# The normaliser multiplied onto q, the KV product added to the lepe sum in PSUM, and the work placed anew

## The chip, the core and the metric

The kernel runs on one core of a Trainium2 chip. A core has TensorE for matrix products (PE in the profile), VectorE (DVE), ScalarE (ACT), GpSimd (POOL) and SyncE (SP), which only issues copies here. SBUF holds operands, PSUM the sums of TensorE. Every engine works through its own list of instructions in order; semaphores connect the lists. The metric is the device time of one execution in microseconds (us).

## The reference

All data is fp32. `x` is [8, 128, 16, 16]: 8 batches, 128 channels, T = 256 positions. Two layers follow each other, each with a group norm before it and a residual around it. The first is linear attention with a gate:

```
q, k, v, o = split(w_qkvo @ gn(x) + b)               # 128 channels each, 8 heads of 16
lepe = depthwise 5x5 conv of v + b_lepe
q, k = elu(q) + 1, elu(k) + 1
k    = k * softmax(mean(q) . k) * T
z    = 1 / (q . mean(k) + 1e-6)
kv   = rope(k)^T v / T
res  = (rope(q) @ kv) * z + lepe
x    = x + w_proj @ (res * o) + b_proj
```

The second is a Mamba block on the normalised x: a projection, a causal convolution over 4 positions, and a selective scan with 16 states for each of 64 inner channels, in four groups of channels:

```
h[t] = exp(delta[t] * A) * h[t-1] + delta[t] * u[t] * B[t];   y[t] = sum over states (h[t] * C[t]) + D * u[t]
x    = x + proj(layernorm(y * silu(z) @ W_out + skip * gn(x)))
```

## The kernel before

The scans set the frame. A batch has 8 units g = 0 to 7, each a tile of 128 x 1024 (4 groups of channels times 256 positions on the free axis). Per unit VectorE forms `DB` = du * Bs in PSUM (L1174) and scans it with the decay `dec` (L1199) into `hst`; GpSimd multiplies `hst` by `Cs` (L958); ScalarE makes `dec` two units ahead from the copies `dlt` (L843); TensorE sums `hst` over the states into Y ("collect", L573 and L583). In the last two batches scan and products run in halves. `du` is spread over the partitions by a matmul (L556) at the start of a batch's units 0 and 4; `Bs`, `Cs` and `dlt` are spread by copies through DRAM scratch that SyncE issues (L264, L272). After unit 7's collect VectorE gates the sum: `y` (L1144), in the middle of the next batch's unit 1.

All the rest of the work is woven into the units. It is written as short generators, one for each stage and engine: `front` (q, k, v, o, softmax, normaliser, rope, KV), `lepe` (the 5x5 convolution, 32 matmuls of L430 on four shifted copies `V` of v), `mid` (result, projection, group norm, layer norm: `xl`, `XN`), `tail` (Mamba projections up to `delta` and `du`), `back` (output projection: `xl2` L1147, X L827, the store L303). While batch b is scanned, `back` runs for b-1, `tail` for b+1, `mid` for b+2, `front` and `lepe` for b+3. A `yield n` in a generator is the place, in quarters of a unit (0 to 31), at which its next step is issued; these numbers alone set the order on each engine. Batches 1 to 4 are a loop of two pairs. For the first batches, which have no period before them, the tables `places` give the positions: below 100 before the first scan, 100 to 132 inside batch 0, above it between batch 0 and batch 1. Steps with equal places keep the order back, tail, mid, front, lepe.

The steps that the change touches: `QR` (L707) is the rotated q, copied from PSUM; `lz` and `zS` (L708, L711) the normaliser 1/(...) as exp(-ln); `KVM` (L1081) the masked KV; L440 multiplies KVM by QR into F1[:, T:2T]; VectorE then forms `u1` (L1090) = that times zS, and `u2` (L1094) = lepe in F1[:, 0:T] + bias + u1; GpSimd gates, `u3` = u2 * o (L922); L444 and L447 add X and the projection in PSUM. On the way to the layer norm of `back`: L536 the sum, L815 its square, L540 the variance, L818/L821 ln and exp (`rr2`), L1147 `xl2`, L544/L546 the output.

Of the kernel before, what the change touches and what calls it, by code (L numbers as in the profile page):

```python
# [7 lines left out]
ALU = mybir.AluOpType  # L8
# [39 lines left out]
def block_kernel(nc, x, w0, w1, cc, out):  # L48
    with ExitStack() as ctx:
# [33 lines left out]
        QR = [sb(f"QR_{j}", [P, T]) for j in range(2)]  # L83
        lz, zS = sb("lz", [P, T]), [sb(f"zS_{j}", [P, T]) for j in range(2)]
        KVT, KVM = sb("KVT", [P, 4, P]), [sb(f"KVM_{j}", [P, P]) for j in range(2)]
        u1, u2, u3 = sb("u1", [P, T]), sb("u2", [P, T]), sb("u3", [P, T])
# [123 lines left out]
        def _(sp):  # L210
# [10 lines left out]
            def front(b, j):  # L221

                yield 6
                sp.wait_ge(S("vpad_ready"), b + 1)
                sp.dma_start(v_dram, vpad[:]).then_inc(S("v_out"), 16)
                yield 17
# [9 lines left out]
            def mid(b, j):  # L236

                yield 21
# [36 lines left out]
            def tail(b, j):  # L275

                yield 17
                sp.wait_ge(S("bc_ready"), b + 1)
                sp.dma_start(bc_dram[j].rearrange("w s (h n) -> h (w s) n", h=2), bc[:]).then_inc(S("bc_out"), 16)
                yield 17  # L280
                spill(b, j)
                yield 18
                load_delta(b, j, 0)
                load_delta(b, j, 1)

            def lead(b, j):

                yield 7
# [3 lines left out]
                yield 26  # L292
# [7 lines left out]
            def back(b, j):  # L300
                yield 31
# [13 lines left out]
            def weights(b, j):  # L315
# [4 lines left out]
                    1: (96.882, 104.059, 111.235,),  # L320
                },
                "lead": {
                    0: (39.471, 46.647,),
                },
                "mid": {
                    0: (3.588,),
                    1: (68.176, 75.353,),
                    2: (118.412, 124,),
                },
                "front": {  # L330
                    0: (10.765, 17.941,),
                    1: (25.118, 32.294,),
                    2: (53.824, 61,),
                    3: (82.529, 89.706,),
# [7 lines left out]
        def _(pe):  # L342
# [14 lines left out]
            def weights(b, j):  # L357
                yield 2
                averages(1, 1, B, F2)
                yield 10  # L360
# [12 lines left out]
            def front(b, j):  # L373
# [6 lines left out]
                yield 9  # L380
# [21 lines left out]
                yield 22  # L402
# [10 lines left out]
                yield 23  # L413
# [5 lines left out]
            def lepe(b, j):  # L419

                for n, (dy, dx) in enumerate(PLACES):
                    yield (20, 20, 23, 24, 28, 31, 31, 31)[n]
# [5 lines left out]
                    for q in range(Q):  # L428
# [3 lines left out]
                                  start=(n == 0), stop=(n == ROUNDS - 1))  # L432
                last.then_inc(S("lepe_done"), 1)

            def mid(b, j):
# [3 lines left out]
                pe.wait_ge(S("qr_ready"), b + 1)  # L439
                mm(F1[:, T:2 * T], KVM[j][:], QR[j][:], start=True, stop=True).then_inc(S("res_done"), 1)  # L440
                yield 7
                pe.wait_ge(S("gms_ready"), 2)
                pe.wait_ge(S("u2_ready"), b + 1)
                mm(F1[:, T:2 * T], wt("ident"), X[:, bass.ds(b, 1), :].rearrange("p b t -> p (b t)"), start=True,  # L444
                   stop=False)
# [7 lines left out]
                yield 17  # L453
# [9 lines left out]
            def tail(b, j):  # L463
# [18 lines left out]
                yield 6  # L482
                pe.wait_ge(S("zs_ready"), b + 1)
                mm(F2[:], wdt[:], flat(xs[j][:]), start=True, stop=True).then_inc(S("dt_done"), 1)
                yield 10
# [3 lines left out]
            def lead(b, j):  # L489

                yield 20
# [15 lines left out]
                yield 26  # L507
# [4 lines left out]
                yield 26  # L512
# [14 lines left out]
            def back(b, j):  # L527
# [3 lines left out]
                yield 16  # L531
# [6 lines left out]
                yield 22  # L538
# [66 lines left out]
            def finish():  # L605
# [3 lines left out]
                for g in range(GROUPS - LAG, GROUPS):  # L609
# [5 lines left out]
                    1: (122.6, 125, 127.333, 128.222,),  # L615
                },
                "lead": {
                    0: (67.073, 71.951, 100.7,),
# [3 lines left out]
                    1: (98.78, 103.5, 104.9, 111.5, 114.5,),  # L622
                    2: (121.8, 127.111, 127.778, 128, 128.444,),
                },
                "lepe": {
# [4 lines left out]
                },  # L630
                "front": {
# [686 lines left out]
```

## Time and profile before

| | us |
|---|---|
| median of 3 runs (375.87 to 378.69) | 376.57 |
| the profiled execution | 374.03 |
| its span | 372.2 |
| busy: TensorE | 274.4 (74%) |
| VectorE | 275.2 (74%) |
| ScalarE | 220.1 (59%) |
| GpSimd | 201.5 (54%) |
| mean granted clock of TensorE | 0.892 of full |

The span is the time from the first to the last instruction; the execution's own time has some start and end around it. A busy share is a mean over stages: before the first scan (at about 60 us), between batch 0 and 1 (about 96 to 121 us) and at the end engines wait for each other in short chains, and in between the scans run.

### The profile page before, as it was taken

To read this page: it belongs to the slowest core of one execution; us is meant where nothing else is said; L and a number is where in the kernel's file an instruction comes from. 1 tells how busy PE (TensorE), PEld (TensorE's weight loads), DVE (VectorE), ACT (ScalarE), POOL (GpSimd) and SP (SyncE) were. 2 spreads that over 40 slices of the span, in tenths; PEclk is the share of its full clock that TensorE was granted. 3 is DMA by queue.
4 is the path that set the end of the run, shared out by engine and by line. 5 is a ranking of instruction groups with operands and counts; after the bars stand their busy time and mean duration, and the time that the engine had idled before them with its cause. 6 is when DMAs were issued, how large, how long until landed. Compare 5 with 4: busy or idle time off the path is not lost.

```text
span 372.2 us, 5571 instructions
## 1 busy us (share of the span) xinstructions
PE 274.4 (74%) x1882; PEld 128.2 (34%) x1882; DVE 275.2 (74%) x342; ACT 220.1 (59%) x408; POOL 201.5 (54%) x135
## 2 busy tenths in 40 slices
PE   2498796797678795977697759776987666964763
PEld 1264343353224242633363335333532212321321
DVE  1622228879410998699968996899699998999992
ACT  2413886566634795669656974698468737552211
POOL 0020201645290389358935893579458876876750
PEclk9999999589958899899989998999899875868598
DMA  7230407832248709960897079706960694196000
GB/s 261 83 87 3 112 15 279 307 77 56 77 129 277 308 30 247 299 234 25 211 314 253 26 211 307 260 23 175 336 268 8 223 295 169 42 344 236 0 14 14
DMA packets 27075, 61.73 MB, mean 166 GB/s; under 512 B 2992, under 2 KB 14896, under 8 KB 27056
## 3 DMA queue, kind: packets, MB, share of 16 engines
q1 hardware_dynamic: 26768, 60.88, 50.8%
q10 hardware_dynamic: 288, 0.61, 0.5%
q8 instruction: 11, 0.18, 0.2%
q14 instruction: 8, 0.07, 0.1%
HBM read 54.62 MB, written 6.86 MB: 165 GB/s over the span
## 4 chain that ended last, share of the span: by engine, by line
PE 26%; DVE 17%; issue 17%; DMA 12%; ACT 12%; POOL 10%; SPq 4%; POOLq 1%; DVEq 0%; ACTq 0%
POOL hst L958 6%; DVE hst L1199 4%; DMA V<-v_scratch 4%; PE F L430 4%; PE Y L583 3%; DVE DB L1174 3%; DVE hst L1186 2%; PE DB L556 2%; DMA Cs<-bc_scratch 2%; DVE DB L1170 2%; SPq L229 2%; PE F L378 2%; PE F L408 2%; DMA CCs<-cc 1%; POOL delta L931 1%
## 5 line engine op out<-in xcount | busy, mean ns | idle before, releaser
L958 POOL TENSOR_TENSOR hst<-hst,Cs 128x1024 f32<-128x1024 f32 x48 | 113.2, 2360 | 80.9 <-DVE hst L1199 80.6
L1199 DVE TENSOR_TENSOR_SCAN hst<-dec,DB 128x1024 f32<-128x1024 f32 x48 | 109.5, 2282 | 1.1
L843 ACT ACTIVATE dec<-dlt,negA 128x1020 f32<-128x1020 f32 x60 | 68.1, 1141 | 13.6 <-DVE hst L1189 9.3
L1174 DVE TENSOR_TENSOR DB<-DB,Bs 128x1024 f32<-128x1024 f32 x48 | 58.9, 1228 | 3.8 <-PE DB L556 1.5
L583 PE MATMUL Y<-hst,CCs 128*32 128x256 f32 x512 | 50.1, 429 | 11.7 <-POOL hst L955 9.5
L430 PE MATMUL F<-V,wpatch 128*32 128x256 f32 x512 | 38.2, 423 | 12.6 <-DMA V<-v_scratch 10.6
L955 POOL TENSOR_TENSOR hst<-hst,Cs 128x512 f32<-128x512 f32 x31 | 38.7, 1269 | 15.9 <-DVE hst L1186 15.9
L583 PEld LDWEIGHTS Y<-hst,CCs 128*32 128x32 f32 x512 | 14.8, 116 | 47.8 <-issue 31.4
L430 PEld LDWEIGHTS F<-V,wpatch 128*32 128x32 f32 x512 | 14.9, 115 | 29.7 <-DMA V<-v_scratch 12.2
L556 PE MATMUL DB<-du,CCs 32*128 32x512 f32 x64 | 21.2, 742 | 4.4 <-DVE DB L1170 3.3
L922 POOL TENSOR_TENSOR u<-u,oS 128x256 f32<-128x256 f32 x8 | 5.8, 724 | 31.3 <-DVE u L1094 31.3
L911 POOL TENSOR_TENSOR tq<-QK,W0s 128x512 f32<-128x512 f32 x8 | 9.0, 1124 | 24.5 <-DVE QK L1076 24.5
L1170 DVE TENSOR_TENSOR DB<-DB,Bs 128x512 f32<-128x512 f32 x32 | 20.5, 686 | 1.1 <-PE DB L556 0.9
L1081 DVE TENSOR_TENSOR KVM<-F,CCs 128x128 f32<-128x128 f32 x8 | 2.3, 285 | 24.3 <-PE F L416 24.1
L1186 DVE TENSOR_TENSOR_SCAN hst<-dec,DB 128x512 f32<-128x512 f32 x16 | 19.4, 1210 | 0.0
L1189 DVE TENSOR_TENSOR_SCAN hst<-dec,DB 128x512 f32<-128x512 f32 x16 | 19.1, 1194 | 0.0
L1147 DVE SCALAR_TENSOR_TENSOR xl<-F,W1s,rr 128x256 f32<-128x256 f32 x8 | 3.8, 480 | 16.4 <-ACT rr L821 16.4
L676 ACT ACTIVATE r_qk<-F,W0s 128x256 f32<-128x256 f32 x16 | 6.7, 470 | 14.4 <-PE F L378 14.4
L408 PE MATMUL F<-CCs,tk 128*128 128x128 f32 x64 | 13.7, 356 | 0.8 <-ACT lz L708 0.8
L408 PEld LDWEIGHTS F<-CCs,tk 128*128 128x128 f32 x64 | 12.7, 267 | 4.3 <-ACT lz L708 2.0
L573 PE MATMUL Y<-xs,dsel 128*32 128x256 f32 x128 | 12.0, 452 | 2.2 <-DVE y L1144 2.0
L479 PE MATMUL F<-XN,W1s 128*32 128x256 f32 x112 | 8.3, 420 | 6.8 <-ACT xs L758 6.8
(176 smaller groups left out, 509.7 us busy)
## 6 DMA issues: line engine op xcount, KB each, us to landing
Bs<-bc_scratch SPq DMA_DIRECT2D x32, 512.0 KB, 5.8
Cs<-bc_scratch SPq DMA_DIRECT2D x32, 512.0 KB, 6.5
dlt<-delta_scratch SPq DMA_DIRECT2D x15, 512.0 KB, 5.8
V<-v_scratch SPq DMA_DIRECT2D x32, 200.0 KB, 4.2
XN<-xn_scratch SPq DMA_DIRECT2D x28, 128.0 KB, 3.1
delta_scratch<-delta SPq DMA_DIRECT2D x16, 128.0 KB, 4.1
v_scratch<-vpad SPq DMA_DIRECT2D x8, 211.5 KB, 2.3
bc_scratch<-bc SPq DMA_DIRECT2D x8, 128.0 KB
```

The costliest lines, as they stand in the source:

```text
L408: mm(F0[:, P * blk:P * blk + P], tk[:, which, P * blk:P * blk + P], wt(turn), start=(which == 0), stop=(which == 1))
L430: last = mm(F1[CM * q:CM * q + CM, 0:T], wpatch[:, ROUNDS * q + n, :], img[:, :, 0:W], start=(n == 0), stop=(n == ROUNDS - 1))
L556: last = mm(DU[:, half, :], wt("pick")[p0:p0 + DD], du[j][p0:p0 + DD, :], start=True, stop=True)
L583: last = mm(Y[CM * i:CM * i + CM, T * kg:T * kg + T], wt("place"), hst[g % 4][:, T * i:T * i + T], start=False, stop=(g % 4 == 3))
L843: af(dec[g % 4][:, :, 1:T], dlt[2 * j + g // SG][:, :, 1:T], ACT.Exp, scale=negA[:, g:g + 1]).then_inc(S("decay_ready"), 1)
L955: tt(part, part, halves(Cs[g % SG], half), ALU.mult).then_inc(S(signal), 1)
L958: tt(hst[g % 4][:], hst[g % 4][:], Cs[g % SG][:], ALU.mult).then_inc(S("hc_ready"), 1)
L1170: v.tensor_tensor(BIN[:, half, :], DU[:, half, :], halves(Bs[g % SG], half), ALU.mult).then_inc(S(signal), 1)
L1174: v.tensor_tensor(flat(BIN), flat(DU), Bs[g % SG][:], ALU.mult).then_inc(S("b_ready"), 1)
L1186: v.tensor_tensor_scan(halves(hst[g % 4], 0), flat(dec[g % 4][:, 0:2, :]), BIN[:, 0, :], 0.0, ALU.mult, ALU.add).then_inc(S("h_half"), 1)
L1189: v.tensor_tensor_scan(halves(hst[g % 4], 1), flat(dec[g % 4][:, 2:4, :]), BIN[:, 1, :], 0.0, ALU.mult, ALU.add).then_inc(S("h_ready"), 1)
L1199: v.tensor_tensor_scan(hst[g % 4][:], flat(dec[g % 4][:]), flat(BIN), 0.0, ALU.mult, ALU.add).then_inc(S("h_ready"), 1)
```

## The change

What is computed stays the same, since z only depends on the position and head of q. GpSimd multiplies the rotated q by the normaliser: `QZ` = QR * zS, a step of `front`. L440 multiplies KVM by QZ and adds itself to the open lepe sum in F1[:, 0:T] (`start=False`), so the lepe rounds no longer close it. VectorE then makes `u3` = (F1 + bias) * o in one operation; `u1` and `u2` are gone, and GpSimd no longer gates. The projection product now comes before the product that adds X. QR and zS have one buffer instead of two, QZ two. And nearly all places have new numbers.

```diff
@@ front, TensorE, ScalarE and SyncE are only placed anew; GpSimd:
+                yield 23
+                pool.wait_ge(S("qr_ready"), b + 1)
+                pool.wait_ge(S("zS_ready"), b + 1)
+                wait(pool, "res_done", b - 1)
+                tt(QZ[j][:], QR[:], zS[:], ALU.mult).then_inc(S("qz_ready"), 1)
@@ lepe, TensorE
-                yield (20, 20, 23, 24, 28, 31, 31, 31)[n]
+                yield (22, 25, 25, 26, 27, 28, 28, 29)[n]
...
-                                  start=(n == 0), stop=(n == ROUNDS - 1))
+                                  start=(n == 0), stop=False)
@@ mid, TensorE
-                pe.wait_ge(S("qr_ready"), b + 1)
-                mm(F1[:, T:2 * T], KVM[j][:], QR[j][:], start=True, stop=True).then_inc(S("res_done"), 1)
-                yield 7
-                pe.wait_ge(S("gms_ready"), 2)
-                pe.wait_ge(S("u2_ready"), b + 1)
-                mm(F1[:, T:2 * T], wt("ident"), X[:, bass.ds(b, 1), :]..., start=True, stop=False)
+                pe.wait_ge(S("qz_ready"), b + 1)
+                mm(F1[:, 0:T], KVM[j][:], QZ[j][:], start=False, stop=True).then_inc(S("res_done"), 1)
+                yield 8
                 pe.wait_ge(S("u3_ready"), b + 1)
-                mm(F1[:, T:2 * T], wt("wproj"), u3[:], start=False, stop=True).then_inc(S("proj_done"), 1)
+                mm(F1[:, T:2 * T], wt("wproj"), u3[:], start=True, stop=False)
+                mm(F1[:, T:2 * T], wt("ident"), X[:, bass.ds(b, 1), :]..., start=False, stop=True)
@@ back, TensorE: the variance matmul
-                yield 22
+                yield 19
                 pe.wait_ge(S("sq2_ready"), b + 1)
@@ front, ScalarE
-                yield 22
+                yield 23
                 act.wait_ge(S("rope_done"), b + 1)
-                wait(act, "u1_ready", b - 1)
-                wait(act, "res_done", b - 1)
-                nc.scalar.copy(QR[j][:], F0[:, T:2 * T]).then_inc(S("qr_ready"), 1)
+                wait(act, "qz_ready", b)
+                nc.scalar.copy(QR[:], F0[:, T:2 * T]).then_inc(S("qr_ready"), 1)
@@ mid, GpSimd
-                pool.wait_ge(S("u2_ready"), b + 1)
-                pool.wait_ge(S("o_ready"), b + 1)
-                tt(u3[:], u2[:], oS[j][:], ALU.mult).then_inc(S("u3_ready"), 1)
+                yield from ()
@@ mid, VectorE
-                v.tensor_tensor(u1[:], F1[:, T:2 * T], zS[j][:], ALU.mult).then_inc(S("u1_ready"), 1)
...
-                v.scalar_tensor_tensor(out=u2[:], in0=F1[:, 0:T], scalar=wt("blepe"), in1=u1[:],
-                                       op0=ALU.add, op1=ALU.add).then_inc(S("u2_ready"), 1)
-                yield 14
+                v.scalar_tensor_tensor(out=u3[:], in0=F1[:, 0:T], scalar=wt("blepe"), in1=oS[j][:],
+                                       op0=ALU.add, op1=ALU.mult).then_inc(S("u3_ready"), 1)
+                yield 12
@@ back, SyncE: the store of the output
-                yield 31
+                yield 25
@@ places of SyncE: the dlt copies of batch 1 are the third number of tail
-                    1: (96.882, 104.059, 111.235,),
+                    1: (102.938, 110.562, 123,),
```

What the numbers do shows best in the order of an engine. TensorE in the second half of a batch in the loop, before (L540 is the variance for xl2, L430 lepe with its copies V, L556 the broadcast of du for the next batch):

```order
L399 MATMUL F<-tq,CCs 128x256 x2
...
L430 MATMUL F<-V,wpatch 32x256 x8
L540 MATMUL F<-sq,CCs 128x256
...
L416 MATMUL F<-KVT 128x128 x2
L430 MATMUL F<-V,wpatch 32x256 x8
...
L544 MATMUL F<-xl,W1s 128x256
...
L430 MATMUL F<-V,wpatch 32x256 x4
...
L556 MATMUL DB<-du,CCs 128x512 x2
...
L430 MATMUL F<-V,wpatch 32x256 x12
```

and with the change (lines 2 lower, so L538 is the variance, L554 the broadcast):

```order
L538 MATMUL F<-sq,CCs 128x256
L394 MATMUL F<-QK,Mk 128x256
L399 MATMUL F<-tq,CCs 128x256 x2
...
L430 MATMUL F<-V,wpatch 32x256 x4
...
L430 MATMUL F<-V,wpatch 32x256 x8
...
L430 MATMUL F<-V,wpatch 32x256 x4
...
L544 MATMUL F<-X,CCs 128x256
L416 MATMUL F<-KVT 128x128 x2
L430 MATMUL F<-V,wpatch 32x256 x12
...
L554 MATMUL DB<-du,CCs 128x512 x2
L430 MATMUL F<-V,wpatch 32x256 x4
```

The variance matmul moved from behind the first lepe round to ahead of all of them, 28 lepe matmuls instead of 20 stand ahead of the broadcast, and 4 instead of 12 behind it.

SyncE between batch 0 and batch 1, before (dlt are the copies from which batch 1's decays are made):

```order
L272 DMA dlt<-delta_scratch 128x1x1024 x2
L242 DMA xn_scratch<-XN 128x259
L264 DMA Bs<-bc_scratch 128x1x1024
L264 DMA Cs<-bc_scratch 128x1x1024
L246 DMA XN<-xn_scratch 32x4x256 x4
```

and with the change:

```order
L242 DMA xn_scratch<-XN 128x259
L264 DMA Bs<-bc_scratch 128x1x1024
L264 DMA Cs<-bc_scratch 128x1x1024
L272 DMA dlt<-delta_scratch 128x1x1024 x2
L246 DMA XN<-xn_scratch 32x4x256 x4
```

The dlt copies moved behind the store of XN and the first pair of Bs and Cs. In the loop's second half of a batch, SyncE with the change:

```order
L246 DMA XN<-xn_scratch 32x4x256 x4
...
L303 ISA
L303 DMA out<-X 128x256
L261 REGISTER_ALU
L264 DMA Bs<-bc_scratch 128x1x1024
L264 DMA Cs<-bc_scratch 128x1x1024
```

Here the store of the output, L303, moved from behind the third pair of Bs and Cs to ahead of the second one.

## Rows read from the trace of the kernel before

**Rows 1.** The page's first line.

```profile
span 372.2 us, 5571 instructions
```

**Rows 2.** VectorE's timeline: start, duration, line, operation, tiles, count, idle time before.

```profile
200.01 0.69 DVE L1144 TENSOR_TENSOR y<-Y,zs 128x512 f32<-128x512 f32 x1 [0.72 <-PE Y L583]
...
206.45 2.28 DVE L1199 TENSOR_TENSOR_SCAN hst<-dec,DB 128x1024 f32<-128x1024 f32 x1
...
226.98 0.48 DVE L1147 SCALAR_TENSOR_TENSOR xl<-F,W1s,rr 128x256 f32<-128x256 f32 x1 [3.73 <-ACT rr L821]
...
233.66 1.23 DVE L1174 TENSOR_TENSOR DB<-DB,Bs 128x1024 f32<-128x1024 f32 x1 [0.36 <-PE DB L556]
...
238.03 0.69 DVE L1144 TENSOR_TENSOR y<-Y,zs 128x512 f32<-128x512 f32 x1 [0.73 <-PE Y L583]
238.63 1.22 DVE L1174 TENSOR_TENSOR DB<-DB,Bs 128x1024 f32<-128x1024 f32 x1
...
274.64 0.67 DVE L1144 TENSOR_TENSOR y<-Y,zs 128x512 f32<-128x512 f32 x1
```

**Rows 3.** Chain of waits, 198 to 240 us: start, duration, engine, tile, line.

```profile
208.81 2.36 POOL hst L958
...
217.73 5.43 DMA V<-v_scratch
```

**Rows 4.** TensorE's timeline, in two neighbouring periods.

```profile
185.19 1.19 PE L430 MATMUL F<-V,wpatch 128*32 128x256 f32 x16 [2.41 <-DMA V<-v_scratch]
...
223.20 1.63 PE L430 MATMUL F<-V,wpatch 128*32 128x256 f32 x16 [2.85 <-DMA V<-v_scratch]
224.76 1.22 PE L540 MATMUL F<-sq,CCs 128*128 128x256 f32 x2
...
232.30 1.13 PE L556 MATMUL DB<-du,CCs 32*128 32x512 f32 x4
...
233.81 1.50 PE L430 MATMUL F<-V,wpatch 128*32 128x256 f32 x24
```

**Rows 5.** Groups by line and form: count, busy us, mean ns, idle before.

```profile
L922 POOL TENSOR_TENSOR u<-u,oS 128x256 f32<-128x256 f32 x8 | 5.8, 724 | 31.3 <-DVE u L1094 31.3
...
L1090 DVE TENSOR_TENSOR u<-F,zS 128x256 f32<-128x256 f32 x8 | 3.3, 415 | 1.8 <-PE F L440 1.8
```

**Rows 6.** SyncE's copies by time of issue.

```profile
108.91 1.21 SPq L272 DMA_DIRECT2D dlt<-delta_scratch  x2
...
227.90 0.52 SPq L264 DMA_DIRECT2D Bs<-bc_scratch  x1
```

**Rows 7.** From issue to landing: of tile Bs, then the page's row of dlt.

```profile
DMA to landing us min/median/max: 3.8/5.8/8.4
...
dlt<-delta_scratch SPq DMA_DIRECT2D x15, 512.0 KB, 5.8
```

**Rows 8.** VectorE's timeline between batch 0 and batch 1.

```profile
121.01 0.29 DVE L1081 TENSOR_TENSOR KVM<-F,CCs 128x128 f32<-128x128 f32 x1 [13.76 <-PE F L416]
...
125.00 0.67 DVE L1144 TENSOR_TENSOR y<-Y,zs 128x512 f32<-128x512 f32 x1
```

**Rows 9.** ScalarE's timeline.

```profile
120.09 0.61 ACT L671 ACTIVATE xg<-X,gms,grs 128x256 f32 x1
120.60 1.14 ACT L843 ACTIVATE dec<-dlt,negA 128x1020 f32<-128x1020 f32 x1
...
231.99 0.47 ACT L827 ACTIVATE X<-F,bout 128x256 f32 x1 [1.25 <-PE F L546]
```

**Rows 10.** TensorE's timeline between batch 0 and batch 1.

```profile
121.36 1.13 PE L378 MATMUL F<-xg,W0s 128*128 128x256 f32 x4 [0.38 <-DVE KVM L1081]
...
123.43 0.64 PE L583 MATMUL Y<-hst,CCs 128*32 128x256 f32 x8
```

**Rows 11.** TensorE by stretch: busy, count, granted clock, share of the DMA engines, GB/s.

```profile
224.00:226.00 2.00, 2.00 (x12) 0.50 0.93 368
226.00:228.00 2.00, 2.00 (x18) 0.75 0.97 328
```

More of the change, by code:

```diff
@@ L82, in block_kernel @@
         tq, tk = sb("tq", [P, 2, T]), sb("tk", [P, 2, T])
-        QR = [sb(f"QR_{j}", [P, T]) for j in range(2)]
-        lz, zS = sb("lz", [P, T]), [sb(f"zS_{j}", [P, T]) for j in range(2)]
+        QR, QZ = sb("QR", [P, T]), [sb(f"QZ_{j}", [P, T]) for j in range(2)]
+        lz, zS = sb("lz", [P, T]), sb("zS", [P, T])
         KVT, KVM = sb("KVT", [P, 4, P]), [sb(f"KVM_{j}", [P, P]) for j in range(2)]
-        u1, u2, u3 = sb("u1", [P, T]), sb("u2", [P, T]), sb("u3", [P, T])
+        u3 = sb("u3", [P, T])
         x1sq, gi, ga, nv, lnv, rs, ms = (sb(n, [P, w]) for n, w in (
@@ L286, in lead @@
             def lead(b, j):
-                yield 7
+                yield 21
                 sp.wait_ge(S("bc_ready"), b + 1)
@@ L319, in _ @@
                 "tail": {
-                    1: (96.882, 104.059, 111.235,),
+                    1: (102.938, 110.562, 123,),
                 },
                 "lead": {
-                    0: (39.471, 46.647,),
+                    0: (41.938, 49.562,),
                 },
                 "mid": {
-                    0: (3.588,),
-                    1: (68.176, 75.353,),
-                    2: (118.412, 124,),
+                    0: (3.812,),
+                    1: (72.438, 80.062,),
+                    2: (118.188, 125,),
                 },
                 "front": {
[L331 to L334, printed above, removed]
+                    0: (11.438, 19.062,),
+                    1: (26.688, 34.312,),
+                    2: (57.188, 64.812,),
+                    3: (87.688, 95.312,),
                 },
@@ L357, in weights @@
             def weights(b, j):
-                yield 2
+                yield 0
                 averages(1, 1, B, F2)
-                yield 10
+                yield 6
                 pe.wait_ge(S("gavg_ready"), 2)
@@ L701, in front @@
                 af(Mk[:], wt("head"), ACT.Copy, scale=ksum[:]).then_inc(S("mk_ready"), 1)
-                yield 22
+                yield 23
                 act.wait_ge(S("rope_done"), b + 1)
-                wait(act, "u1_ready", b - 1)
-                wait(act, "res_done", b - 1)
-                nc.scalar.copy(QR[j][:], F0[:, T:2 * T]).then_inc(S("qr_ready"), 1)
+                wait(act, "qz_ready", b)
+                nc.scalar.copy(QR[:], F0[:, T:2 * T]).then_inc(S("qr_ready"), 1)
                 af(lz[:], F0[:, 0:T], ACT.Ln, bias=wt("zeps")).then_inc(S("lz_ready"), 1)
-                yield 22
+                yield 25
                 act.wait_ge(S("lz_ready"), b + 1)
-                af(zS[j][:], lz[:], ACT.Exp, scale=-1.0).then_inc(S("zS_ready"), 1)
+                wait(act, "qz_ready", b)
+                af(zS[:], lz[:], ACT.Exp, scale=-1.0).then_inc(S("zS_ready"), 1)
                 yield 25
@@ L862, in weights @@
             def weights(b, j):
-                yield 3
+                yield 18
                 deviations(1, 1, B)
-                yield 12
+                yield 23
                 act.wait_ge(S("w0_loaded"), 16)
@@ L966, in _ @@
                 "tail": {
[L967 to L972 removed]
+                    1: (136.2, 148.6,),
                 },
                 "front": {
[L975 to L978 removed]
+                    0: (8.5, 25.5, 42.5,),
+                    1: (59.5, 76.5, 93.5,),
+                    2: (111, 113, 120,),
+                    3: (161, 173.4, 185.8,),
                 },
@@ L1036, in weights @@
                                     S("wpatch_ready"), 1)
-                yield 4
+                yield 1
                 moments(1, 1, B)
-                yield 7
+                yield 3
                 variances(1, 1, B, F2)
-                yield 7
+                yield 6
                 offsets(1, 1, B)
-                yield 7
+                yield 6
                 v.tensor_tensor(wtap[:], wt("wxp"), wt("convw"), ALU.mult)
```

164 lines of the change are left out of this document (75 added, 89 removed), and 30 rows, old and new, of the table places.

## The prediction

> **What bounds the kernel now.** The profiled execution took 374.03 us, 372.2 of it span [rows 1]. The median of the three runs shown is 376.57, so it was a quick one; I sum against it and carry the difference over to the median.
>
> I read the page first, then VectorE's timeline, because the scans run there. Batches 1 to 4 each take about 37.5 us from one gated sum `y` (L1144) to the next: y stands at 125.00 [rows 8] and, four periods on, at 274.64 [rows 2]. The period from 200.01 to 238.03 is worked out here. VectorE idles in it 3.73 us before `xl2` (L1147), 0.36 before the next batch's first product `DB` and 0.73 before `y` [rows 2]. Only the first looks large, and it is tempting to take it as the bound. The chain of waits says otherwise: in the same stretch it runs from GpSimd's product after scan 2 to the copies of `V` and then into TensorE [rows 3]. TensorE's own timeline shows why: it sits 2.85 us before L430, released by the copies of `V`, and is then busy without a gap through the broadcast of `du` (L556) and the collects after it [rows 4]. So a period is a loop of four legs:
> - y to the end of scan 2: 8.72 us (200.01 to 206.45 + 2.28) [rows 2];
> - end of scan 2 to V: 14.4 (208.73 to 217.73 + 5.43 = 223.16) [rows 2, 3];
> - V to the end of the du broadcast: 10.2 (223.20 to 232.30 + 1.13) [rows 4];
> - from there to the next y: 4.6 (to 238.03) [rows 2].
>
> Sum 37.9. `xl2` is late only because its variance matmul L540 is queued behind the L430, at which TensorE waits for V.
>
> **The change, part by part.** (1) VectorE loses L1090, 415 ns [rows 5], and gains nothing: L1094 becomes one operation of the same form, which gates as well. The rows of neighbours overlap by some 0.07, so I take 0.35. It lies between y and the end of scan 2: the loop gets 0.35 shorter.
>
> (2) GpSimd loses the gate L922, 724 ns, and gains one product of that size [rows 5]. The product stands after that of unit 5, where GpSimd waits for scan 6, the scan that came only after the wait for `xl2` [rows 2]. Cost nothing while scan 6 is what GpSimd waits for; if that cover goes, 0.72 per period.
>
> (3) The KV product goes into the lepe sum: same matmul, same place in the order. The projection now puts `wproj` before the identity product, which thus follows `u3` instead of preceding it. The loop doesn't run through either: 0.
>
> (4) TensorE's order is the main term. The profile counts two passes per matmul. From V to L556 there stood 20 matmuls of L430, L540 and the rest; now L540 is gone from there (1.22 us) and there are 28 of L430. Twelve of them fill 1.50 [rows 4], so eight more cost 1.0 to 1.1: the leg gets 0.15 shorter. Behind the broadcast 12 of L430 become 4, so -1.0, of which y can give back the 0.73 that it waited [rows 2, 4]. Together -0.35 - 0.15 - 0.75 = **-1.25 us per period**, four periods: **-5.0**.
>
> (5) The 3.73 us before `xl2` go, since L540 now stands before L394 and waits only for its square. I count nothing for it. VectorE reaches the next batch's `DB` that much sooner and waits there for L556, which hangs on V: the stall moves. Its bounds are 0 (V decides) and -3.7 per period (VectorE decides); I take 0, since the chain passes through V [rows 3]. `ga` now stands before scan 3 and its matmul L451 later; I estimate 0.9 us of delay for scans 3 to 7, inside the 3.7 to spare.
>
> (6) SyncE. The store of the batch's output, which waits for L827, goes ahead of the second Bs/Cs pair, issued at 227.90 before [rows 6]. L827 ended at 232.46 [rows 9]; with L544 and L546 sooner in TensorE's order I estimate 231, the pair at 231.4, so 3.5 later. Its reader started at 238.63 [rows 2] and will near 237.3: 5.9 us later, and the median from issue to landing is 5.8, the slowest 8.4 [rows 7]. I take 0; bounds 0 and +2.5 per period.
>
> (7) Between batches 0 and 1 VectorE stands 13.76 us before `KVM`, until 121.01, and y comes at 125.00 [rows 8]. The new order takes 24 matmuls of L430 out of the way of L394 and L399, so KVM could come several us sooner, I estimate near 116. But the dlt copies, issued at 108.91 [rows 6], now stand behind the store of XN and the first Bs/Cs pair, which wait for bc. Following the order I get them issued at about 111, landed 5.8 later [rows 7]; then two decays of 1.14 and xg0 (0.61) on ScalarE [rows 9]; L378 to the collect's end, 2.7 (121.36 to 123.43 + 0.64) [rows 10]; y near 123.3. I take -1.5. Bounds: -4.5 (only KVM decides) and +2.1 (the copies' delay is passed on whole). The work before the first scan gets perhaps 1 us shorter, which ends in the same wait and isn't counted again.
>
> (8) Batch 5 loses L1090 and a little wait before y: **-0.5**. Batches 6 and 7 have no attention work left: 0.
>
> Sum: -1.5 - 5.0 - 0.5 = -7.0. Profiled execution 367.0; median 376.57 - 7.0 = **369.6**, the likeliest case's own range 367 to 372.5.
>
> **The rivals.** *TensorE keeps its clock.* Behind the wait for V the granted clock is 0.50, which is the 1.2 GHz level, for two us and 0.75 on average for two more [rows 11]; at full speed that work would take 1.0 + 0.5 = 1.5 us less. The wait ahead of it gets shorter, since L540 and a later `Mk` fill it: by my count 1.6 instead of 2.85. If the clock then stays up, 1.5 x 4 = 6.0 more are saved: 363.6. For it: less idling. Against: one period before, the wait was only 2.41 and the matmuls behind it ran no faster [rows 4]. The Trainium skill (TensorE: Matmul & The Clock Gate, section HAM oscillation) says that waits for DMA between bursts of matmuls are what lets the clock fall; by that rule the order with less idle time is the faster one. Chance 0.27.
>
> *VectorE decides after all.* If nobody waits for the du broadcast, the wait before xl2 and L1090 are saved whole: -(3.73 + 0.35) x 4 - 2 = -18.3, 358. The chain speaks against it. Chance 0.05.
>
> *The gain is eaten: the change doesn't do what it says.* The wait before xl2 turns into one for L556 that is as long or longer, since collects and the K products, moved between the L430, now wait for GpSimd (its `tk` comes one product later), in a stretch that had no gap; and (7) gives nothing or takes. About 375.5. Chance 0.17.
>
> *The Bs/Cs copies come late (slower).* SyncE stands at L303 until L827 is done, with the second and third pair behind it. At the slowest landing of 8.4 [rows 7] VectorE waits 2.5 us before its second DB in each of six batches: 15 - 7 = +8, 384.6. It turns to slower from 7.0 / 6, about 1.2 us of lateness per batch on. For it: the DMA engines are 0.93 to 0.97 busy there [rows 11]. Against: little is queued ahead by then. The Trainium skill (DMA: Bandwidth & Descriptors, section Queues, rings and completion order) says that on each DMA engine the descriptors of one issuer are taken in ring order. [...] Chance 0.08.
>
> **How the numbers follow.** 369.6 with 0.43; clock kept 363.6, 0.27; VectorE decides 358, 0.05; eaten 375.5, 0.17; slower 0.08. A measurement of this kernel tells about 1% from no change: 372.8 to 380.3. Faster 0.43 + 0.27 + 0.05 = 0.75, same 0.17, slower 0.08. The range, 362 to 375.5, leaves out the slower case, half of the eaten one, and what lies below the kept clock.
>
> **What would show it.** Right: no wait before xl2, and in its place 2 to 4 us before DB, released by the du broadcast, in four periods; y to y 36 to 36.6; batch 0's y near 123; TensorE still waiting for V. Wrong: a period below 35.5 (clock, or VectorE decides); DB waiting for Bs, or the first decay for dlt, over 1 us; gaps in TensorE between V and the broadcast.

## The result and the profile after

| | before | after |
|---|---|---|
| median, first session | 376.22 (4 runs, 375.70 to 378.69) | 362.24 (4 runs, 358.12 to 365.83) |
| ratio, 95% interval | | 0.9596 (0.9523 to 0.9669) |
| three later sessions, three chips | 373.56, 375.29, 374.09 (23, 17, 11 runs) | 365.50, 365.12, 364.07 (6 runs each) |
| their ratios (95% intervals) | | 0.9749 (0.9686 to 0.9812), 0.9749 (0.9696 to 0.9802), 0.9711 (0.9638 to 0.9783) |
| profiled execution, its span | 374.03, 372.2 | 365.83, 364.0 |
| mean granted clock of TensorE | 0.892 | 0.861 |

The change makes the kernel faster: by 4.0% in the first session, by 2.5 to 2.9% in the later ones. The forecast was 1.9%. The profiled executions differ by 8.2 us, while the first medians differ by 14.0: the one of after was its slowest of four, that of before the quickest seen in its session. The sizes below therefore come from the traces of several sessions: four of the changed kernel, one of the kernel before. Executions of one kernel scatter by some 8 us, and the ratios compare only those within 1.5% of that kernel's quickest.

VectorE's timeline after, one period of the loop (a period runs from one `y` to the next) and the end of the next, with the `y` (now L1135) that [rows 2] shows at 200.01 and 238.03; columns as there:

```profile
159.89 0.67 DVE L1135 TENSOR_TENSOR y<-Y,zs 128x512 f32<-128x512 f32 x1
...
165.98 2.28 DVE L1190 TENSOR_TENSOR_SCAN hst<-dec,DB 128x1024 f32<-128x1024 f32 x1
...
184.73 0.47 DVE L1138 SCALAR_TENSOR_TENSOR xl<-F,W1s,rr 128x256 f32<-128x256 f32 x1
...
191.71 1.23 DVE L1165 TENSOR_TENSOR DB<-DB,Bs 128x1024 f32<-128x1024 f32 x1 [0.54 <-PE DB L554]
...
195.26 0.67 DVE L1135 TENSOR_TENSOR y<-Y,zs 128x512 f32<-128x512 f32 x1
...
227.38 1.23 DVE L1165 TENSOR_TENSOR DB<-DB,Bs 128x1024 f32<-128x1024 f32 x1 [2.23 <-PE DB L554]
```

The 3.73 us before `xl2` are gone, and VectorE waits for the du broadcast before `DB` instead, 0.54 and 2.23 here. This period is 35.37, where the forecast had 36 to 36.6; the four of this trace are 36.23, 35.37, 35.68 and 35.29. TensorE's timeline (first two of these rows from the period of 145, then 182) shows the reason:

```profile
145.76 0.64 PE L430 MATMUL F<-V,wpatch 128*32 128x256 f32 x8 [2.00 <-DMA V<-v_scratch]
...
154.97 1.13 PE L554 MATMUL DB<-du,CCs 32*128 32x512 f32 x4
...
182.73 0.64 PE L430 MATMUL F<-V,wpatch 128*32 128x256 f32 x8 [0.41 <-DMA V<-v_scratch]
...
190.34 1.13 PE L554 MATMUL DB<-du,CCs 32*128 32x512 f32 x4
```

From V to the end of the broadcast it takes 10.34 in the first (154.97 + 1.13 - 145.76) and 8.74 in the second. The work is the same; the clock is not. TensorE by stretch (busy, count, granted clock, share of the DMA engines, GB/s), behind V in either period, then ten us ahead of V in the second, and last the loop as a whole, in the kernel before and in the changed one:

```profile
147.80:149.80 2.00, 2.00 (x18) 0.50 1.03 409
...
182.70:184.70 2.00, 1.97 (x36) 1.00 1.06 376
...
172.00:174.00 2.00, 2.00 (x5) 0.50 0.04 6
```

```profile
124.00:266.00 142.00, 112.07 (x832) 0.94 0.63 197
```

```profile
124.00:266.00 142.00, 117.60 (x918) 0.94 0.66 207
```

At 0.50 TensorE has its 1.2 GHz level, 18 records in 2 us, and at 1.00 the 2.4 GHz level, 36. The third row says where the clock is low in the second period: ten us before V. TensorE is busy there at half clock, but it has time to spare, for it still waits 0.41 for V afterwards. The clock of the loop as a whole is 0.94 in both kernels (0.91 to 0.92 in the other three traces of the changed one), so what counts is where the low stretches lie. The mean of the span fell from 0.892 to 0.861 mainly outside the loop: from 0.81 to 0.76 in 60 to 124 us and from 0.80 to 0.74 in 266 to 358.

The four legs of the loop, each worked out as for the period from 200.01, now over all four periods of every trace (us; V to broadcast lists each period):

| | y to scan 2 | scan 2 to V | V to broadcast | broadcast to y | four periods |
|---|---|---|---|---|---|
| before | 8.72 | 13.9 to 14.5 | 10.23 x4 | 4.59 x3, 3.56 | 149.6 |
| after | 8.37 | 13.7 to 14.8 | 10.34, 8.74, 8.77, 8.76 | 3.79 x3, 3.52 | 142.6 |
| e1, e8, e17 (the same kernel) | 8.37 | 13.5 to 15.4 | 10.41 once, 8.75 eleven times | 3.79, 3.6 | 142.2, 139.5, 141.3 |

In 12 of the 16 periods of the changed kernel TensorE still waits for V. In the other four it comes to V without a wait, and in one of them this costs time. In e17 the clock was 0.50 from 204 to 212, TensorE was busy there without a gap, and it came to V at 216.13, 15.37 behind scan 2, where the other three periods have 13.8 to 14.5:

```profile
216.13 0.64 PE L430 MATMUL F<-V,wpatch 128*32 128x256 f32 x8
```

Between batch 0 and batch 1, VectorE, then ScalarE, then TensorE, after:

```profile
111.23 0.29 DVE L1076 TENSOR_TENSOR KVM<-F,CCs 128x128 f32<-128x128 f32 x1 [6.38 <-PE F L416]
112.84 1.23 DVE L1165 TENSOR_TENSOR DB<-DB,Bs 128x1024 f32<-128x1024 f32 x1 [1.32 <-DMA Bs<-bc_scratch]
...
117.44 2.29 DVE L1190 TENSOR_TENSOR_SCAN hst<-dec,DB 128x1024 f32<-128x1024 f32 x1 [3.37 <-ACT dec L841]
...
123.66 0.69 DVE L1135 TENSOR_TENSOR y<-Y,zs 128x512 f32<-128x512 f32 x1 [3.93 <-PE Y L581]
```

```profile
116.11 2.18 ACT L841 ACTIVATE dec<-dlt,negA 128x1020 f32<-128x1020 f32 x2 [5.96 <-DMA dlt<-delta_scratch]
```

```profile
118.92 2.07 PE L378 MATMUL F<-xg,W0s 128*128 128x256 f32 x4 [5.84 <-ACT xg L669]
121.22 1.80 PE L470 MATMUL F<-XN,wtap 128*64 128x512 f32 x4 [0.23 <-DMA XN<-xn_scratch]
```

`KVM` comes 9.8 us sooner than in [rows 8], and y only 1.3. VectorE's one wait of 13.76 has turned into waits for KVM, Bs, dec and y, and TensorE works at half clock behind its own (L378 took 1.13 in [rows 10]).

### The profile page after: what moved, and what is told of

Read it like the earlier page. It is cut to its first block, busy times and chain, and to the rows that moved or that the text cites. A ratio compares the mean times of both kernels' runs of the same rounds, so it can differ in the third digit from the quotient of the medians.

```text
span 364.0 us, 5551 instructions
## 1 busy us (share of the span) xinstructions
PE 273.2 (75%) x1882; PEld 130.7 (36%) x1882; DVE 272.0 (75%) x334; ACT 218.2 (60%) x408; POOL 201.7 (55%) x135
## 4 chain that ended last, share of the span: by engine, by line
PE 30%; DVE 20%; DMA 16%; POOL 9%; issue 9%; ACT 9%; SPq 6%; POOLq 0%; DVEq 0%; ACTq 0%
DVE hst L1190 7%; PE F L430 6%; POOL hst L958 6%; DMA V<-v_scratch 6%; PE DB L554 3%; DVE DB L1165 3%; DMA bc_scratch<-bc 3%; PE Y L581 3%; DVE hst L1177 3%; DVE DB L1161 3%; DMA Cs<-bc_scratch 2%; SPq L253 2%; PE F L408 2%; DVE hst L1180 2%; SPq L229 2%
## 5 line engine op out<-in xcount | busy, mean ns | idle before, releaser
L581 PE MATMUL Y<-hst,CCs 128*32 128x256 f32 x512 | 52.0, 453 | 10.8 <-POOL hst L955 7.0
L430 PE MATMUL F<-V,wpatch 128*32 128x256 f32 x512 | 34.8, 395 | 5.0 <-DMA V<-v_scratch 5.0
L554 PE MATMUL DB<-du,CCs 32*128 32x512 f32 x64 | 24.7, 855 | 4.7 <-DVE DB L1161 4.0
L430 PEld LDWEIGHTS F<-V,wpatch 128*32 128x32 f32 x512 | 14.8, 110 | 20.5 <-DMA V<-v_scratch 6.7
L384 PE MATMUL F<-xg,W0s 128*128 128x256 f32 x32 | 10.7, 465 | 11.3 <-DVE kraw L1059 11.3
L485 PE MATMUL F<-xs,W1s 128*64 128x512 f32 x14 | 9.7, 780 | 11.8 <-DVE cor L1108 11.8
L378 PE MATMUL F<-xg,W0s 128*128 128x256 f32 x32 | 10.8, 467 | 9.0 <-ACT xg L669 8.5
L712 ACT COPY KVT<-F 128x512 f32<-128x512 f32 x8 | 4.7, 583 | 18.6 <-PE F L410 18.6
L1076 DVE TENSOR_TENSOR KVM<-F,CCs 128x128 f32<-128x128 f32 x8 | 2.2, 278 | 15.3 <-PE F L416 15.3
L927 POOL TENSOR_TENSOR dl<-lnu,cor 128x512 f32<-128x512 f32 x7 | 8.9, 1270 | 7.1 <-DVE cor L1108 7.1
```

Of the source, the lines that this page charges most:

```text
L430: last = mm(F1[CM * q:CM * q + CM, 0:T], wpatch[:, ROUNDS * q + n, :], img[:, :, 0:W], start=(n == 0), stop=False)
L554: last = mm(DU[:, half, :], wt("pick")[p0:p0 + DD], du[j][p0:p0 + DD, :], start=True, stop=True)
L581: last = mm(Y[CM * i:CM * i + CM, T * kg:T * kg + T], wt("place"), hst[g % 4][:, T * i:T * i + T], start=False, stop=(g % 4 == 3))
```

## The experiments

Ratios are to the kernel before, on the same chip.

**e1, e8, e17: the changed kernel again.** No edit.

> The changed kernel once more, unchanged. Its own profiled execution was 365.83 us, 8.2 below that of the kernel before, while its median was 14 below. Theory (the loop through V, with the clock as its second term): batches 1 to 4 take 35.3 to 35.7 us from y to y wherever TensorE's granted clock stays at 1.00 behind the wait for V, 36.2 where it falls to 0.50; quick executions differ from slow ones by how many stretches at 0.50 lie on the path, so an execution of 358 to 361 shows no more than one of the four periods at 36.2 and an earlier y of batch 0. Rival (the quick executions are quicker everywhere): all legs of the period are shorter, also those on VectorE and GpSimd alone. Expected median 361, 359 to 363.

> The changed kernel once more, for its time beside these and a third profile. If the first session's ratio of 0.960 was one end of the scatter, this one lies near the second session's 0.975: 363 to 367, clock at 1.00 behind V in three of the four periods, total of the legs -7 to -8 against before. If the first was typical: ratio 0.965 or below, and a profiled execution of 362 or less.

> The changed kernel beside it: 365, ratio 0.975, batch 0's y at 125 to 128. If the first session's 0.960 is typical of some chips and this is one: both kernels lower, the old tables still 2 to 3 us below.

Measured: 365.50, 365.12, 364.07 (table above). In all four traces, with spans from 359.2 to 364.6, y to scan 2 is 8.36 to 8.39, and V to broadcast is either 10.3 to 10.4 or 8.75, by the clock. The rival that all is quicker falls. But the clock behind V is not all that sets a quick execution apart: e17's trace is 5.4 us shorter than e1's, 3.35 of it by an earlier y of batch 0 (122.53 for 125.88) and only 1.0 in the four periods. Nothing near the first session's 0.960 came again for this kernel.

**e2 and e3: the places alone, the data flow alone.** e2 is the kernel before with the new numbers (`u1`, `u2` at 5 and 6 and GpSimd's gate at 8 keep their steps), e3 the changed kernel with the old numbers (`u3` at 6, `QZ` at 23).

> Nearly all new places, with the old data flow (u1, u2, gate on GpSimd). Theory (the gain is the new order): it keeps all but the 0.35 us per batch of the removed VectorE operation and GpSimd's gate: 2 to 3 us above the changed kernel, about 363, ratio to before 0.965. Rival (the gain is the new data flow, places only follow it): 370 or more, ratio 0.985 or above. Expected 363, 360 to 367.

> The new data flow (QZ on GpSimd, KV product into the lepe sum, the gate with the bias on VectorE) at the old places. Theory: only the 0.35 us of L1090 per batch of 1 to 5 goes, about -1.8: 374.4, ratio 0.995. Rival (data flow decides): -6 or more, ratio under 0.985. Rival (GpSimd's product, which has to wait for zS and stands ahead of the product of unit 6, delays the scans' products): +1 to +3, ratio above 1.0.

Measured: e2 372.51 (365.81 to 374.55) against 373.56, a scatter too wide for a ratio; e3 372.92, ratio 0.9950 (0.9905 to 0.9995). By the medians neither half alone is worth over 1 us or so, and together, in the same session, they are worth 8. The traces say less: e2's profiled execution took 368.90, well below its median, and its four periods take 144.6, 5.0 below before, with the clock kept behind V in all of them. What the places alone are worth is therefore not settled. e3 is as expected in time, though the clock behind V was kept in two of its four periods: in these V to broadcast is 8.62, but scan 2 to V is 15.3 instead of 13.6 to 13.7, since the clock was 0.50 ahead of V (170 to 180 in the period from 159.63) and TensorE came to V late. Moving the low stretch from behind V to right ahead of it gained nothing here. Where e2 loses time against the changed kernel stands in its trace, on GpSimd, TensorE and VectorE:

```profile
130.08 2.35 POOL L958 TENSOR_TENSOR hst<-hst,Cs 128x1024 f32<-128x1024 f32 x1 [7.54 <-DVE hst L1199]
132.39 0.72 POOL L922 TENSOR_TENSOR u<-u,oS 128x256 f32<-128x256 f32 x1
```

```profile
133.16 1.22 PE L447 MATMUL F<-u,W0s 128*128 128x256 f32 x2 [1.84 <-POOL u L922]
134.18 1.91 PE L384 MATMUL F<-xg,W0s 128*128 128x256 f32 x4
```

```profile
139.40 0.16 DVE L1098 COPY ga<-F 128x2 f32<-128x2 f32 x1 [3.65 <-PE F L451]
```

The gate stands behind a full product of `hst` on GpSimd. L447 waits for it, and behind L447 in TensorE's order stands L384, which makes v and so V: scan 2 to V is 16.44 us in this period and 15.54 in a later one, and `ga`, placed early, waits 3.65. My reading is that the new order can move these steps forward because the gate no longer passes through GpSimd. It is not shown: L447 waits 1.85 in the period from 163.02 too, where the leg is 14.26, and in the first period L384 also ran at half clock (1.91 for 1.03).

**e4, e7, e10: the variance matmul.** e4 moves it alone, e10 takes it back; e7, meant as e10, put it at 22, which is still ahead of V.

```diff
 e4, the kernel before, back, TensorE
-                yield 22
+                yield 19
                 pe.wait_ge(S("sq2_ready"), b + 1)
 e10, the changed kernel (e7: 22)
-                yield 19
+                yield 24
                 pe.wait_ge(S("sq2_ready"), b + 1)
```

> The kernel before with one number changed: the variance matmul of the last layer norm stands at place 19 instead of 22 in TensorE's order, ahead of the wait for V. Theory (loop through V): VectorE no longer waits 2.9 to 3.7 us before xl2, but waits as long before the next batch's DB; the leg from V to the du broadcast loses the 1.22 us of the matmul: -1.2 x 4 = -4.9, 371.3, ratio 0.987; with the clock kept behind V 1.0 to 1.5 per period more, down to 366, ratio 0.973. Rival (VectorE decides, the wait before xl2 is itself the loss): -3.4 x 4 = -13.4, 363, ratio 0.964. Rival (nothing but a wait moved): 1.0.

> The changed kernel with the variance matmul (L538) back at place 22, behind V and the first lepe round. Theory (that matmul fills the wait for V and takes work out of the leg behind it): the wait for V back at 2 to 3 us, the clock at 0.50 behind it in at least three of four periods, V to du broadcast 10.5 to 10.8 instead of 8.75, xl2 waits 2 us or more; periods +1.6 to +2.0, total +5 to +8 over the changed kernel: ratio to before 0.99 to 1.00. Rival (lepe's places and the shorter chain of the gate carry the gain, the variance does not matter): within 1.5 us of the changed kernel, ratio 0.975 to 0.98.

> The changed kernel with the variance matmul (L538) truly behind V: behind the first 8 matmuls of L430 and a collect. (Place 22, tried before, left it ahead of V.) Theory of the forecast: 0.54 to 1.1 us more in the leg from V to the du broadcast (9.3 with the clock kept, 10.8 without), wait for V longer by 0.5 and so the clock lost in more periods, xl2 waiting again 1 to 3 us: total +2 to +7 over the changed kernel, ratio to before 0.98 to 0.99. Rival (the matmul's place does not matter, since the scans' side has the time to spare): within 1.5 us of the changed kernel, ratio 0.975.

Measured: e4 371.76 us, ratio 0.9929 (0.9885 to 0.9973), e7 364.28 us, ratio 0.9732 (0.9677 to 0.9787), e10 0.9897 (0.9836 to 0.9958), 372.13 us. In e4 the clock fell behind V in all four periods, and V to broadcast is 9.79, only 0.44 below before, not 1.22. I read this so: other matmuls took the place of the one removed in the stretch at half clock, so that it saved about what it costs at full clock (0.5 to 0.7 in other rows). No run tests that reading. In e10, TensorE and VectorE:

```profile
183.62 0.64 PE L430 MATMUL F<-V,wpatch 128*32 128x256 f32 x8 [2.05 <-DMA V<-v_scratch]
...
185.85 1.22 PE L538 MATMUL F<-sq,CCs 128*128 128x256 f32 x2
...
193.58 1.13 PE L554 MATMUL DB<-du,CCs 32*128 32x512 f32 x4
```

```profile
188.57 0.48 DVE L1138 SCALAR_TENSOR_TENSOR xl<-F,W1s,rr 128x256 f32<-128x256 f32 x1 [4.05 <-ACT rr L819]
```

V to broadcast is 9.75 in the one period with the clock kept and 11.1 in the three without: 1.0 for the matmul's place (0.17 of it a wait for ScalarE) and 1.35 for the clock, with periods of 37.5. Where the clock falls, the place is worth 0.7 (11.1 for 10.34 to 10.41). This one number, undone, takes back more than half of the gain. e7 says nothing on it.

**e5: V early.** The V copies go ahead of the spills in SyncE's order, in the kernel before.

```diff
 front, SyncE
-                yield 17
+                yield 16
                 sp.wait_ge(S("v_out"), 16 * (b + 1))
```

> The kernel before with the four copies of V issued ahead of the spills of bc and delta in the loop, right when v has landed in DRAM (in the period from 200.01 they were issued at 215.16, v landed at about 212.8). Theory (the loop of batches 1 to 4 runs through V): V comes 2.4 us sooner, the waits of 2.4 to 2.85 us before L430 almost go, V follows no longer from scan 2, periods 1.6 to 3.6 us shorter, the total 6 to 12 below: about 365, ratio 0.975. With less idling ahead of L430 the granted clock behind it may stay at 1.00, which is 1.6 per period of the gain. Rival (V is not what decides; collects, the K products and VectorE end the period at the same time): within 1% of before, 371 to 377, the wait turning up before L408 or before KVM. Rival (later spills of bc and delta delay dlt and Bs): slower.

Measured: 371.65 us, ratio 0.9834 (0.9772 to 0.9897). Scan 2 to V fell from 14.1 to 11.0 to 12.1, no period waits for V any more, V to broadcast is 8.62 in all. So V decided the legs up to it. The whole fell short of the 0.975 expected, for broadcast to y rose from 4.6 to between 6.3 and 9.7, and the four periods together take 147.2, only 2.4 below before. Another transfer is late now (TensorE, e5):

```profile
263.07 1.50 PE L430 MATMUL F<-V,wpatch 128*32 128x256 f32 x24
269.33 1.98 PE L472 MATMUL F<-XN,wtap 128*64 128x512 f32 x4 [4.75 <-DMA XN<-xn_scratch]
```

The store of XN stands in SyncE's queue behind the dlt copies, which wait for the delta spill, issued later here.

**e6 and e9: a filler ahead of the wait for V.** In the kernel before the rope product of q is done three times over, with the same result, in all batches (e6) or in the loop alone (e9).

```diff
 front, TensorE
+                for again in range(1 if isinstance(b, int) else 3):
                     for which, turn in enumerate(("ident", "rot")):
```

> The kernel before with the rope product of q (L399) done three times over, same result: TensorE has 2.06 us more work just ahead of its wait for V, all of it inside that wait (2.4 to 2.85 us). It separates the clock from the order. If idling ahead of L430 is what lets the granted clock fall behind it: the wait becomes 0.4 to 0.8, the clock stays at 1.00, the leg from V to the du broadcast falls from 10.23 to 8.6, periods -1.6, total -6: ratio 0.983. If the clock falls at a time that has nothing to do with that wait: legs as before, ratio 1.00, with the fall in the same number of periods.

> The kernel before with the rope product of q done three times in the loop alone (batches 0 to 3, which come before the loop, do it once). The filler in all batches gave periods of 36.12, 35.40, 36.15 and 35.85, with no fall of the clock behind V, but cost about 4 us ahead of batch 0's y. Theory (the clock behind V is worth 1.6 us per period, and idling ahead of it is what costs it): y of batch 0 near 125, four periods together -6, total -6: ratio 0.984. Rival (the falls only move, to batches 5 and 6 where they cost the same): ratio 0.995 or above, with batch 5 at 33 us or more.

Measured: e6 374.01 us, ratio 0.9956 (0.9914 to 0.9998), its four periods 143.5 us (-6.1), batch 0's y 4.2 later, which is why the 0.983 expected did not come. e9 0.9859 (0.9808 to 0.9911), 368.93 us, -5.2; its four periods take 143.9 (-5.7). TensorE in e9, then by stretch:

```profile
214.68 2.75 PE L400 MATMUL F<-tq,CCs 128*128 128x256 f32 x12
218.53 1.08 PE L431 MATMUL F<-V,wpatch 128*32 128x256 f32 x16 [1.09 <-DMA V<-v_scratch]
...
226.01 1.13 PE L557 MATMUL DB<-du,CCs 32*128 32x512 f32 x4
```

```profile
218.00:220.00 2.00, 1.47 (x18) 1.00 0.78 312
220.00:222.00 2.00, 2.00 (x28) 1.00 0.66 108
```

More work, and 8.61 instead of 10.23 from V to broadcast, in all four periods. This shows the clock's share apart from any order: 1.6 us per period. The rival came in part: batch 5 took 33.75 us instead of 31.66, with the clock at 0.57 from 276 to 280, where it was 1.00 before. The Trainium skill (TensorE: Matmul & The Clock Gate, section HAM oscillation) blames waits for DMA between bursts; here the traces agree, since filling the wait for V kept the clock at 1.00. The waits in that section's example are 3 to 5 us; here shorter ones were followed by a fall. Over the 76 periods of all 19 traces, the clock fell behind V after 15 of the 16 waits for V of 1.94 us or more, and after none of the 60 that were shorter or missing. The length of that wait alone does not decide: the clock fell behind 2.05 in e10 and held behind 2.09 in the changed kernel. What differs between these was not tried.

**e11: lepe's places.** The changed kernel with `(20, 20, 23, 24, 28, 31, 31, 31)` again for the eight rounds of L430.

> The changed kernel with the old places of the lepe matmuls: 20 of them ahead of the du broadcast and 12 behind it, instead of 28 and 4. The forecast had the leg V to broadcast pay 1.0 us for the eight more, and the leg from broadcast to y give 0.75 back. Theory: 7.75 + 4.6 = 12.35 instead of 8.75 + 3.79 = 12.54: nothing to lose or gain, 0 to -1 us in total, ratio 0.973 to 0.976, y waiting 0.7 for the collect. Rival (the collect behind the broadcast is what decides): periods 0.8 longer, +3, ratio 0.983.

Measured: 365.88 us, ratio 0.9738 (0.9685 to 0.9792); V to broadcast 7.85, broadcast to y 4.59. In three of the four periods their sum is 12.44 against 12.54: moving lepe gives nothing.

**e12, e13: fillers in the changed kernel.** The lepe matmuls of batch 2 done three times and the rope product twice in the odd periods (e12); the lepe matmuls of batch 3 done twice (e13).

> The changed kernel with fillers on TensorE where it idles and the clock falls on the path: the 32 lepe matmuls of batch 2 done three times (3.9 us more, in the 5.8 us before L378 between batch 0 and batch 1), and the rope product twice in batches 1 and 3 of the loop. Theory: L378 and L470 at full clock, batch 0's y 1.7 sooner (123.4 instead of 125.1 to 125.9), period 1 at 35.2 in all executions: -2 to -3 against the changed kernel, 362, ratio 0.968. Rival (the fall comes all the same, or later where it costs as much): ratio 0.975.

> The changed kernel with the 32 lepe matmuls of batch 3 done twice between batch 0 and batch 1, right before TensorE waits 4.1 to 5.8 us for xg0 (L378). They take 3.6 to 3.8 us, so all of it lies in that wait. (The filler tried before stood elsewhere, ahead of batch 1's gate at 87 us, and made the path 7 us longer.) Theory: the clock stays at 1.00, L378 takes 1.13 instead of 2.07, L470 1.08 instead of 1.98; L470 waits for XN all the same until 122.1 to 122.8, so batch 0's y comes 1.0 to 1.8 sooner: ratio 0.971 against 0.975. Rival (the fall costs nothing there, since XN's copies decide): y sooner by less than 0.5, ratio 0.975.

Measured: e12 0.9891 (0.9804 to 0.9977): I had placed the first filler wrongly, at 87 us, where it took 7.24 us on the path, and y of batch 0 came at 129.71. Its four periods take 140.5, inside the changed kernel's 139.5 to 142.6, so the second filler shows nothing either. e13 0.9740 (0.9707 to 0.9773). TensorE, e13:

```profile
116.84 3.70 PE L438 MATMUL F<-V,wpatch 128*32 128x256 f32 x64
121.12 1.13 PE L378 MATMUL F<-xg,W0s 128*128 128x256 f32 x4 [0.58 <-ACT xg L677]
123.93 1.71 PE L478 MATMUL F<-XN,wtap 128*64 128x512 f32 x4 [1.69 <-DMA XN<-xn_scratch]
```

L378 is quick again, and the time goes into the wait for XN (y at 126.71, not sooner): the fall costs nothing there.

**e14: dlt first.** In the changed kernel the third place of SyncE's `tail` for batch 1 is 118 instead of 123, which puts the dlt copies ahead of XN's store again.

> The changed kernel with the dlt copies of batch 1 issued ahead of XN's store and the first Bs/Cs pair, as in the kernel before; nothing else. Term 7 took -1.5 for the stretch between batch 0 and 1, with dlt late by 2. Theory: dlt lands 1 us sooner at most (delta's spill lands near 109), the first decays and xg0 follow, L378 0.5 to 1 sooner, XN and Bs 1.2 later; batch 0's y within 0.7 of the changed kernel: ratio 0.973 to 0.978. Rival (the lateness of dlt is passed on whole): y 2 sooner, ratio 0.970. Rival (XN's copies, now later, decide): y 1 later, ratio 0.978.

Measured: 366.30 us, ratio 0.9789 (0.9765 to 0.9813). L378 starts at 117.42 at full clock, but XN is now the late one, y at 126.39:

```profile
123.33 1.98 PE L470 MATMUL F<-XN,wtap 128*64 128x512 f32 x4 [4.79 <-DMA XN<-xn_scratch]
```

**e15, e16: the old tables.** The changed kernel with the tables `places` of all engines as before (for steps that are new: `QZ` at 42.5, 93.5, 120, 185.8 on GpSimd, `u3` at the old places of `u2`).

> The changed kernel with the old tables of places, that is everything ahead of batch 1 in the old order, and the loop and the last batches in the new one. Theory: the loop carries the gain, -1.25 per period by the order and -1.6 by the clock; batch 0's y at 122.6 to 125 as in the kernel before, periods 34.5 to 35.7: total within 1.5 us of the changed kernel, ratio 0.972 to 0.979. Rival (the new tables carry part of the gain): y of batch 0 later than 126, ratio 0.983 or above. Rival (they cost): y at 122.6, ratio 0.968.

> The changed kernel's data flow and loop with the old tables of places, once more, beside the changed kernel on the same chip. Theory (the new tables cost 2 to 3 us, the loop carries more than the whole gain): 362 to 363, ratio 0.967, batch 0's y at 122.6 to 125, clock kept behind V in at least three periods. Rival (the earlier run was a good session): 365, ratio 0.975.

Measured: 362.14 us, ratio 0.9668 (0.9633 to 0.9704), and 362.55, ratio 0.9704 (0.9650 to 0.9758), beside 364.07 (0.9711) for the changed kernel on that chip. The four periods take 140.8 and 139.7. TensorE in e15, where nothing waits for XN or xg0:

```profile
119.81 1.13 PE L378 MATMUL F<-xg,W0s 128*128 128x256 f32 x4 [0.38 <-DVE KVM L1076]
120.87 1.08 PE L470 MATMUL F<-XN,wtap 128*64 128x512 f32 x4
```

The loop carries the whole gain: y of batch 0 stands at 123.44 and 124.94, near the 125.00 of before. That the old tables are better by 1 to 3 us is likely; side by side the difference of 1.5 lies within the intervals.

## Why the prediction was wrong, point by point

**The bound: right in the main.** The loop through V decides. Taking away the wait for V shortened the legs up to it (e5), and what the leg from V to the broadcast loses or gains comes back in the period: -1.6 per period in e9 and -5.7 in its four, +7.2 in e10's four legs against the changed kernel's mean and +7.3 in its periods. In four of 16 periods of the changed kernel TensorE comes to V without a wait, and then its own order ahead of V decides.

**Where it failed: step (4), which priced the leg from V to the broadcast at the half clock of [rows 11], and left the kept clock to a rival with a chance of 0.27.** For the rival I had a wait of 1.6 instead of 2.85; against it I set the neighbouring period, where the wait was 2.41. That argument was weak. The rows I pointed to show those L430 faster, 1.19 for 1.63; it is the whole leg that was as long, 10.23 in both. And it says nothing of a wait of 1.6: in no trace did the clock fall behind a wait of up to 1.85. In the four traces of the changed kernel the clock is kept in 14 of 16 periods, and the leg is 8.75 there instead of the forecast 10.08. The loop gave 7.1, 7.4, 10.1 and 8.4 us instead of 5.0, on average 8.2, and by legs, four periods together:

| | forecast | measured, mean of four traces |
|---|---|---|
| y to scan 2 | -1.4 | -1.4 |
| scan 2 to V | 0 | +0.6 |
| V to broadcast | -0.6 | -5.1 |
| broadcast to y | -3.0 | -2.4 |

The rival's price of 1.5 per period was nearly right (1.6 in e9), and its sign, a period below 35.5, came in 12 of the 16.

**The rest of step (4).** The broadcast-to-y leg gave 0.8 in three of four periods (forecast 0.75) and nothing in the fourth, which was 3.56 before and is 3.5 to 3.6 after. But the price was booked wrongly: the lepe move is zero between the two legs (e11), and it is the variance matmul's place that pays, 1.0 per period with the clock kept (e10), 0.7 and 0.44 where it falls (e10, e4), for which I had booked its 1.22 at half clock.

**Step (1), right:** y to scan 2 8.72 to 8.37. **Step (2), half right:** no row shows `QZ` costing anything in the loop, but taking the gate off GpSimd may not be free of effect: without it the loop gained 5.0 in e2's trace, not 8.2. I had not asked what the gate's place allowed. **Step (3), (6): right,** in none of the four traces does the loop wait for Bs (SyncE's second pair went out 2.4 later in the period on average, 1.5 to 4.1, for the 3.5 forecast), and the slower rival has no row. **Step (5), right in kind:** the wait before xl2 went, and came again before DB, but as 0.2 to 2.4 and in 13 of 16 periods, where I had 2 to 4 in all.

**Step (7), -1.5:** y at 123.66, but 125.88, 125.11 and 122.53 in the other traces: -0.7 on average against 125.00. The mechanism was other than forecast. KVM came at 111, not 116. dlt was the first wait, 3.9 to 6.0 before the first decay in the four traces, which my list had as a sign of being wrong from 1 us on; the first DB waited 1.32 for Bs as well. XN's copies were the wait behind it, so that neither dlt earlier (e14) nor the clock (e13) gives anything. The earlier first scan (its DB at 57.95 for 60.49) ends in the same wait, as I had it. **Step (8), -0.5:** batch 5 took 32.1, 32.4, 33.7 and 31.6 us against 31.66: nothing gained. Batch 6, from y to y, fell from 31.45 to between 29.4 and 29.6 in three traces of four, which I had at 0; the cause of that was not tried.

With these the changed kernel lies 8 to 10 below, as the three later sessions have it, against the forecast 7.0. The 14 of the first session stay open: its interval reaches 0.967, its four executions of after (358.12 to 365.83) lie low beside 18 later ones (360.89 to 368.46), and no trace of a 358 exists.

## What to carry to other kernels

Where TensorE waits in a loop for a transfer and the granted clock falls behind it, the clock is a term of the sum like any other: price the leg at both levels, ask of an edit whether it puts work into that wait, and look where the low stretch goes instead (e3, e9). The cheapest test is a filler that repeats harmless work there (e9: three matmul pairs for one, 1.4% faster). Places and data flow may be worth more together than apart, so try both halves alone and read their traces beside their medians (e2). Judge the start-up order and the loop apart, since here the loop had all of the gain.

## What the runs showed of the hardware that I had not expected

The mean granted clock can fall while the kernel gets faster: 0.861 for 0.892 over the span, and 0.94 in the loop both times, where the gain is; what changed there is where the low stretches lie. The same kernel's executions lie up to 8 us apart on one core (361.55 to 368.46 in e1, 370.49 to 378.67 before); the traces put part of that in which stretches are at 0.50. The Trainium skill (TensorE: Matmul & The Clock Gate, section What's actually happening) says of the warm-up that it differs from run to run, and puts its penalty under 1% of a typical span. For the falls inside the loop the traces show the same kind of difference, one behind V in two traces of the changed kernel and none in the other two. But these recur: in the kernel before, the falls behind V alone were worth 1.4% (e9).
